# Expert layer of a two-layer vision tower: all experts for every token, or tokens sorted by expert into 73 blocks

## What is computed

```python
def _L1_ffn_ref(x, W_qkv, b_qkv, W_gate, b_gate, W_experts, b_experts):   # D = 256, E = 8, TOP_K = 2
    qkv = (x @ W_qkv + b_qkv).reshape(B, S, 3, H, hd)
    attn_out = softmax(q @ k / sqrt(hd)) @ v
    gate = jax.nn.softmax(x @ W_gate + b_gate, axis=-1)
    top_g, top_i = jax.lax.top_k(gate, TOP_K)
    combine = jnp.sum(jax.nn.one_hot(top_i, E) * top_g[..., None], axis=2)
    expert_out = jnp.einsum('bsd,edf->bsef', x, W_experts) + b_experts
    moe_out = jnp.einsum('bsef,bse->bsf', expert_out, combine)
    return attn_out + moe_out
h = h + _L1_ffn_ref(_layernorm(h), ...)
```

## Time and profile before

| what | value |
|---|---|
| median of 3 runs | 2212.42 us (2212.3 to 2214.53) |
| the profiled execution | 2215.91 us, its span 2214.1 us |
| mean granted PE clock | 0.957 |
| PE / DVE / ACT / POOL busy | 2060.5 / 1603.9 / 901.8 / 737.7 us |
| `pass_moe` | 1321 to 1736 us of the span |
| `pass_attend` | 1736 us to the end |

### The profile page before, as it was taken

The page is one execution under the profiler, slowest core; times in us unless marked ns, Lnnn a source line. Parts: engine busy times, 40 slices in busy tenths (PEclk is TensorE's granted clock), DMA queues, the critical chain, the costliest instruction groups (busy, mean ns, idle before and its releaser), DMA issues. The chain is left out here.

```text
span 2214.1 us, 36468 instructions
## 1 busy us (share of the span) xinstructions
PE 2060.5 (93%) x11553; PEld 1337.2 (60%) x11553; DVE 1603.9 (72%) x4388; ACT 901.8 (41%) x2108; POOL 737.7 (33%) x1355
## 2 busy tenths in 40 slices
PE   7997989998999998999979849999999999999997
PEld 5886753335888885777743227888888433333332
DVE  3335977774777767999948846767676888888881
ACT  1113655552112214444424411222222167777777
POOL 3553645553333332333311101111111523333332
PEclk9997989998999999999989969999999789999999
DMA  4332769872000000000010001121217213333310
GB/s 131 114 104 53 176 161 201 165 160 64 1 1 1 1 1 15 1 1 1 1 57 9 10 28 39 40 49 39 49 40 169 43 35 78 78 79 78 78 45 20
DMA packets 212523, 133.86 MB, mean 60 GB/s; under 512 B 113370, under 2 KB 201604, under 8 KB 212356
## 3 DMA queue, kind: packets, MB, share of 16 engines
q1 hardware_dynamic: 212356, 131.78, 25.4%
HBM read 89.96 MB, written 41.38 MB: 59 GB/s over the span
## 5 line engine op out<-in xcount | busy, mean ns | idle before, releaser
L2693 DVE TENSOR_REDUCE attend_mx<-ps 128x1 f32<-128x512 f32 x512 | 320.8, 681 | 40.3 <-PE ps L2387 39.2
L2530 ACT ACTIVATE attend_w<-ps 128x512 f32<-128x512 f32 x512 | 280.5, 596 | 92.6 <-PE ps L2401 91.1
L2003 PE MATMUL ps<-keep_early,moe_zT 128*128 128x256 f32 x1056 | 243.5, 384 | 4.4 <-DVE keep_h L2158 4.4
L2003 PEld LDWEIGHTS ps<-keep_early,moe_zT 128*128 128x128 f32 x1056 | 196.5, 191 | 40.0 <-DVE keep_h L2158 15.5
L2387 PE MATMUL ps<-keep_x,keep_o 96*128 96x512 bf16 x512 | 208.0, 411 | 7.2 <-DVE attend_mx L2693 5.3
L2401 PE MATMUL ps<-keep_o,keep_x 99*128 99x512 bf16 x512 | 191.6, 384 | 2.7 <-ACT attend_w L2530 2.7
L2158 DVE SCALAR_TENSOR_TENSOR keep_h<-ps,moe_g,keep_h 128x256 f32<-128x256 f32 x264 | 127.6, 483 | 61.6 <-PE ps L2003 53.7
L2387 PEld LDWEIGHTS ps<-keep_x,keep_o 96*128 96x128 bf16 x512 | 50.1, 98 | 183.3 <-DVE attend_mx L2693 136.1
L1003 DVE SCALAR_TENSOR_TENSOR keep_early<-ps,first_causal 128x512 f32<-128x512 f32 (+3 forms) x256 | 113.7, 484 | 48.0 <-PE ps L885 43.6
L981 POOL TENSOR_TENSOR keep_early<-keep_early,first_causal 128x128 f32<-128x128 f32 x256 | 113.2, 458 | 86.5 <-ACT keep_early L949 85.5
L1216 PE MATMUL ps<-mlp_zT,keep_early 128*128 128x128 f32 x1056 | 129.1, 281 | 8.0 <-ACT mlp_zT L1258 8.0
(11 more groups left out here) (341 smaller groups left out, 4110.0 us busy)
## 6 DMA issues: line engine op xcount, KB each, us to landing
tok_xin<-in_xk SPq DMA_DIRECT2D x64, 256.0 KB, 2.7
qk_parts<-qkv_parts SPq DMA_DIRECT2D x33, 384.0 KB, 3.2
qk_parts<-moe_parts SPq DMA_DIRECT2D x33, 384.0 KB, 3.2
keep_o<-qk_parts SPq DMA_DIRECT2D x16, 384.0 KB, 4.7
keep_x<-qk_parts SPq DMA_DIRECT2D x16, 384.0 KB, 5.8
v_all<-qkv_v SPq DMA_DIRECT2D x33, 136.0 KB, 3.3
v_all<-moe_v SPq DMA_DIRECT2D x33, 136.0 KB, 3.2
keep_early<-v_all SPq DMA_DIRECT2D x16, 272.0 KB, 6.8
```

The source lines that it names most:

```text
L2003: last = nc.tensor.matmul(ps[:, E0 + pair % 2, e % 2 * D:(e % 2 + 1) * D], zT[:, u, k * P:(k + 1) * P], we[e][:, k, :], start=(k == 0), st ...
L2530: nc.scalar.activation(w[:, j, kt % 2, :], ps[:, SC + (HG * k + j) % RING, :], ACT.Exp)\
L2693: nc.vector.tensor_reduce(mx[:, t, k:k + 1], ps[:, MX + (TB * k + t) % RING, :], AX, ALU.max)\
```

## The change

`pass_moe` no longer multiplies a tile with all experts. Per tile DVE finds the two largest logits and their experts (`rank`, `choose`), `weigh` keeps the two softmax weights in `env.gates`. PE counts, with triangular bf16 matrices, how many tokens before this one chose the same expert (`count`, `totals`), and DVE makes from it two row numbers in a table in DRAM, `sorted` (`places`). POOL issues two indirect transfers a tile that write the normalized rows there (`scatter`). The pipeline has four tiles in hand instead of two, and six buffers of normalized rows. After the last tile DVE works out, on one partition, for each of 73 slots its expert and its first row (`slots`). Then the 73 blocks of 128 rows are done in order: SP reads the row number into a register and loads the block, PE transposes it, DVE copies it to SBUF, ACT reads the expert's number and copies that expert's weights to a fixed place, PE multiplies, DVE reads the number too and adds the expert's bias, and SP stores the result over the block. In `pass_attend` POOL gathers each token's two result rows, weights them and adds them to `env.h`, two tiles a unit. In `pass_fp4` SP writes zeros over the whole table (44,160 rows of 1 KB) in three transfers. The loads of the attention stage are issued at tiles 13, 17, 21 and 25 (`LATE = 20`). The biases of the experts are loaded as one 1 MB transfer, replicated over the partitions, at the start of the stage.

```diff
@@ pass_fp4, SP
             env.ahead["scan"].start(sp)
+            sp.wait_ge(s_blank, 1)
+            runs = io["sorted"].rearrange("(p n c) d -> p n (c d)", p=P, c=BLANK)
+            n = runs.shape[1] // 3
+            zero = env.x[:, 0:BLANK, :].rearrange("p (a c) d -> p a (c d)", a=1)
+            for i in range(3):
+                sp.dma_start(runs[:, i * n:(i + 1) * n, :], zero.to_broadcast([P, n, BLANK * D])).then_inc(env.s_blank_z, 16)
@@ pass_moe
+CAP = (NT + 1) * P
+NSLOT = 2 * NT + E - 1
+ROWS = E * CAP + NSLOT * P
...
+    NZ, NW, NY = 6, 2, 3
...
@@ pass_moe, SP, after the loop over tiles
+            sp.wait_ge(s_slots, 1)
+            for i in range(NZ):
+                sp.wait_ge(s_scat[i], 32 * ((NT - i + NZ - 1) // NZ))
+            def fetch(j, row):
+                past(sp, s_dT, j - NY + 1)
+                sp.dma_start(zs[:, j % NY, :], io["sorted"][bass.ds(row, P), :]).then_inc(s_zs[j % NY], 16)
+            def put_back(j, row):
+                sp.wait_ge(s_y, j + 1)
+                sp.dma_start(io["sorted"][bass.ds(row, P), :], y[:, j % NY, :]).then_inc(s_yout[j % NY], 16)
+            rows = []
+            for j in range(NSLOT):
+                rows.append(sp.value_load(slot_row[0:1, j:j + 1], min_val=0, max_val=ROWS - P))
+                fetch(j, rows[j])
+                if j >= NY:
+                    put_back(j - NY, rows[j - NY])
...
@@ pass_moe, PE
-                for pair in range(3):
-                    experts(s, u, pair)
-                turn_gates(s, u)
-                experts(s, u, 3)
...
-                expert_bias(s)
+            for i in range(NT + 4):
+                if live(i):
+                    transposes(i)
+                if live(i - 1):
+                    gate(i - 1)
+                if live(i - 3):
+                    project(i - 3)
+                if live(i - 2):
+                    count(i - 2)
...
+                if i - 4 >= 1:
+                    class_scores(i - 4)
+            def turn(j):
+                pe.wait_ge(s_zs[j % NY], 16 * (j // NY + 1))
+                past(pe, s_dz, j - 1)
...
+            def expert(j):
+                pe.wait_ge(s_dz, j + 1)
+                pe.wait_ge(s_dW, j + 1)
+                past(pe, s_y, j - 1)
...
+            turn(0)
+            for j in range(NSLOT):
+                if j + 1 < NSLOT:
+                    turn(j + 1)
+                expert(j)
...
@@ pass_moe, ACT
+            for j in range(NSLOT):
+                e = act.value_load(slot_e[0:1, j:j + 1], min_val=0, max_val=E - 1)
+                past(act, s_dM, j - NW + 1)
+                nc.scalar.copy(w_now[:, j % NW, :, :].rearrange("p k d -> p (k d)"),
+                               we[:, bass.ds(e, 1), :].rearrange("p a f -> p (a f)")).then_inc(s_dW, 1)
...
@@ pass_moe, POOL
+            for i in range(NT + 3):
+                if live(i + 2):
+                    deviation(i + 2)
+                if live(i - 3):
+                    third(i - 3)
+                if live(i - 2):
+                    scatter(i - 2)
...
@@ pass_moe, DVE
+            for i in range(NT + 4):
+                if live(i - 1):
+                    rank(i - 1)
+                if live(i - 3):
+                    value(i - 3)
+                if live(i - 1):
+                    choose(i - 1)
+                if live(i + 2):
+                    stats(i + 2)
+                if live(i - 1):
+                    weigh(i - 1)
+                if live(i - 2):
+                    places(i - 2)
+                if live(i + 2):
+                    apply(i + 2)
+                if i - 2 == NT - 1:
+                    slots()
+                if live(i - 3):
+                    split(i - 3)
...
+            turned(0)
+            for j in range(NSLOT):
+                if j + 1 < NSLOT:
+                    turned(j + 1)
+                result(j)
...
@@ pass_attend, POOL, per unit
                 if x.has(1):
                     parts(x)
                     class_weights(x)
+                owed = [i for i in (2 * x.s, 2 * x.s + 1) if i < NT]
+                for i in owed:
+                    fetch(i)
                 if x.follows():
                     add(2 * x.n(2) - 1, 1, x.b(3), 2 * x.half(3) + 1)
                 if x.has(2):
                     add(2 * x.n(2), 0, x.b(2), 2 * x.half(2))
+                for i in owed:
+                    if x.has(2):
+                        pool.wait_ge(s_o, 2 * x.n(2) + 1)
...
+                    combine(i)
```

More of the change, by code:

```diff
@@ L1944, in pass_moe @@
-        s_E, s_acc, s_TC, s_cT, s_be, s_beh, c_g = (a.sem(n) for n in ("E", "acc", "TC", "cTs", "be", "beh", "c_g"))
-        s_out, s_vout = a.sems("out", 2), a.sems("vout", 2)
-        block = a.block()
-        GL, LATE = 9, 6
+        lg = a.sb("lg", [P, E])
+        top = a.sb("top", [P, E])
+        below = a.sb("below", [P, 2, E])
+        ex = a.sb("ex", [P, 2, E])
+        total = a.sb("total", [P, 2])
+        which = a.sb("which", [P, E], U32)
+        which_f = a.sb("which_f", [P, 2])
@@ new lines, in pass_moe @@
+        chosen = a.sb("chosen", [P, 3, 2, E], BF16)
+        place = a.sb("place", [P, 2, E])
+        place_f = a.sb("place_f", [P, 2])
+        tri = a.sb("tri", [P, 2, P], BF16)
+        start = a.sb("start", [1, 1, E], BF16)
+        one = a.sb("one", [1, P], BF16)
+        full = a.sb("full", [1, E, NT])
+        blocks = a.sb("blocks", [1, 3, E])
+        order = a.sb("order", [1, E, E])
+        room = env.heads.room
+        after = room.rearrange("p a t -> p (a t)")[0:1, 0:2 * NSLOT * E].rearrange("p (n j e) -> p n j e", n=2, e=E)
@@ new lines, in pass_moe @@
+        rs = a.sb("rs", [P, 2])
+        ve = a.sb("ve", [P, 2])
+        s_fold, s_kq, s_kq0, s_in = (a.sem(n) for n in ("fold", "kqs", "kq0", "in"))
+        s_stat, s_rs, s_z, c_ln, c_rs = (a.sem(n) for n in ("stat", "rss", "zs_", "c_ln", "c_rs"))
+        s_T, s_zT, s_g, s_mx, s_ex, s_qk, s_v, s_qkf, s_p0, s_rest, s_p1, s_p2, s_va, s_c, s_cs = (
+            a.sem(n) for n in ("T", "zTs", "gs", "mx", "exs", "qk", "vs", "qkfs", "p0", "rests", "p1", "p2", "va", "c", "cs"))
+        s_lg, s_chosen, s_count, s_place, s_all, s_n, c_g, c_w, c_p, c_n = (
+            a.sem(n) for n in ("lgs", "chosens", "count", "places", "all", "n", "c_g", "c_w", "c_p", "c_n"))
@@ L1963, in _ @@
                     env.heads.load_class(sp, io)
-                if 0 <= unit < 4:
-                    env.heads.load(sp, io, unit // 2, unit % 2, unit)
+                if unit >= 0 and unit % 4 == 0 and unit < 16:
+                    env.heads.load(sp, io, unit // 8, unit // 4 % 2, unit // 4)
+            sp.wait_ge(s_slots, 1)
[13 more added lines that the diff above has]
+                    put_back(j - NY, rows[j - NY])
+            for j in range(NSLOT - NY, NSLOT):
+                put_back(j, rows[j])
+            for i in range(NY):
+                sp.wait_ge(s_yout[i], 16 * ((NSLOT - i + NY - 1) // NY))
             for u in range(2):
@@ L2087, in third, with scatter @@
                     .then_inc(s_p2, 1)
[L2089 to L2094, removed]
+            def scatter(s):
+                pool.wait_ge(s_place, s + 1)
+                for j in range(2):
+                    nc.gpsimd.indirect_dma_start(io["sorted"], bass.IndirectOffsetOnAxis(ap=pos[:, s, j:j + 1], axis=0),
+                                                 z[:, s % NZ, :], None).then_inc(s_scat[s % NZ], 16)
+            pool.wait_ge(env.s_blank_z, 48)
+            for s in range(2):
+                deviation(s)
+            for i in range(NT + 3):
+                if live(i + 2):
[4 more added lines that the diff above has]
+                    scatter(i - 2)
         @block.vector
@@ L2132, in gate, with split @@
-                dve.sem_inc(s_comb, 1)
-            def split(s, u):
+            def split(s):
+                u = s % 2
                 dve.wait_ge(s_p0, s + 1)
```

382 lines of the change are left out of this document (253 added, 129 removed).

## The result

| | before | after |
|---|---|---|
| median, 4 runs each | 2213.3 us | 2299.1 us (2298.3 to 2300.2) |
| ratio, 95% interval | 1 | 1.0388 [1.0370, 1.0406] |
| span, mean granted clock | 2214.1 us, 0.957 | 2296.5 us, 0.914 |
| PE / DVE / ACT / POOL busy | 2060.5 / 1603.9 / 901.8 / 737.7 us | 1987.3 / 1541.6 / 934.9 / 949.0 us |

What follows compares the result with a forecast made beforehand. PE bound the 415 us expert stage, busy 403.7. New stage 233 + 5.3 + 5.3 + 157 + 3 = 403.5 us, 11.5 less; +4.7 elsewhere; net -7 from 2212.4 gives 2205 us, range 2140 to 2260.

Steps and rivals of the forecast that it cites:

- The beat of a tile: Expert stage, tile part: 6.2 us a tile, set by POOL's loop with DVE, 33 tiles making 205 us.
- a beat over 7.5: Sign set for a wrong prediction: a tile beat of under 5 or over 7.5 us.
- PE falls to its lower level there: Rival, block part: PE at its lower clock sets the beat at 2.7 us, total 2245 us; chance 0.18.
- 3.8 + 2T: Tile beat from POOL's loop with DVE: 3.8 us plus two scatters of T each, T taken as 1.2 us.
- The rival with scatters of 2.0 us: Slower rival, tile part: each scatter costs 2.0 us, 53 us more, total 2258 us; chance 0.13.
- that with 0.5: Faster rival: scatters of 0.5 us and row-number reads of 0.3 us, 61 us less, total 2144 us; chance 0.22.
- DVE's 4.9: Tile part: DVE's summed work a tile, 4.9 us, said not to set the beat.
- The table: Between tiles and blocks: 13 dependent DVE steps on one partition working out the blocks, 5.3 us.
- The block beat: Block part: three blocks share a round trip of 6.45 us, so 2.15 us a block, 73 blocks making 157 us.
- L = 1.0: Block part: SP's reading of a row number into a register takes 1.0 us.
- Attention: Attention stage: POOL's gathers and sums fit its idle gaps, costing 2 us in the first units; stage 434 +- 3 us.
- a unit over 27.2 us: Sign set for a wrong prediction: a longer attention unit would mean POOL's gaps don't hold the gathers.

Runs made afterwards that it cites:

- experiment 1: Changed kernel with VectorE's take_class(i-5) moved from the end to the start of its iteration: 2185.4 us, 0.9868 of the kernel before.
- experiment 2: Changed kernel with the class scores in two PSUM banks in turn, the copy staying last on VectorE: 2184.6 us, 0.9873 of the kernel before.
- experiment 5: Changed kernel with six more unread 128x256 products a tile on TensorE ahead of the class scores: 2227.2 us.
- experiment 3: Changed kernel without the two scatters of each tile, take_class left last: 2309.3 us.
- experiment 4: Changed kernel with take_class(i-5) first on VectorE and without the two scatters of each tile: 2164.0 us.
- experiment 7: Changed kernel with POOL's first combine of an attention slot put ahead of its second addition: 2290.2 us, 1.0339 of the kernel before.
- experiment 6: Changed kernel with four block buffers instead of three: 2288.5 us, 1.0331 of the kernel before.
- experiment 10: Changed kernel with take_class first, four block buffers, first combine between the additions, and block stores issued by GpSimd: 2148.2 us, 0.9706 of the kernel before.

## Why the prediction was wrong, step by step

- **The beat of a tile: failed, and it decides.** The step is "Neither sets the beat, because POOL now also issues two scatters a tile and its order ties it into a loop with DVE." I had added up PE's 4.3 to 4.7 us and DVE's 4.9 us as if they ran side by side, and had looked for a loop only where the change put a new operation. The loop between PE and DVE goes over the one bank of the class scores, an operation that the change did not touch, only moved: on PE to `i - 4`, on DVE to the end. I had asked of the scatters who waits behind them and had not asked it of the copy. What the runs showed in its place is a beat of 10.24 us, set by PE and DVE in turn; of the signs that I had set, a beat over 7.5 came true. The loop cost 4.16 us a beat: 114.7 us by the two tile parts (349.4 and 234.7), 114 and 115 by the medians of experiments 1 and 2. No rival of mine had it.
- **Its clock.** Of that, experiment 5, a single run, puts some 72 us to the lower level. My rival "PE falls to its lower level there" had the mechanism and the wrong place: in the blocks, where I had been afraid of it, the clock was 0.97.
- **3.8 + 2T and T: right.** The two scatters took 2.5 us with their gaps, a T of 1.25 for my 1.2, and the rest of the loop 3.6 for my 3.8: a beat of 6.08 for 6.2, once the other loop was out; experiments 3 and 4 show that POOL's loop binds only then. The rival with scatters of 2.0 us is out, and so is that with 0.5.
- **DVE's 4.9: near, in part by luck.** The beat of experiment 4 was 5.14 us with DVE busy for 4.9 of it, but 0.6 of that is one small step that POOL's third part holds up (below). Without it my sum was 0.6 too high.
- **The table: right**, 1647.7 to 1653.1, 5.4 us for 5.3.
- **The block beat: right in kind, mis-sized in two terms.** Three blocks do share a round trip, but it took 5.3 us (three beats of 1.77) and not 6.45: the landing 2.1 for my 3.0, and the row read with its address 0.77 for my L = 1.0. The 0.5 that I had taken off for what DVE's read hides stands on no row, and no run shows it. The Trainium skill (DMA: Bandwidth & Descriptors, Latency and other measured facts) gives a `tensor_load`, which is what the read is in the trace, a floor of about 0.6 us. The trace does not bear that out: 72 of SP's 73 reads took 0.27 to 0.29 us, the first 1.07, and the steps on registers behind a read 0.48. The part came 26 us shorter than forecast, 137.2 for 163. The loads behind the stores in SP's queue were no slower: both landed in about 2 us.
- **Attention: mis-sized, and from other causes.** The 434 us that I gave for the stage are the length of the window of the earlier trace rows; the stage lasts 477.6. I had forecast +2 at its start and there were +13.4. The start cost 0.6: the first split comes at 1836.85, 31.4 us into the stage against 25.5 before, but the second follows after 21.1 us instead of 26.3. The 14 units behind it cost 10.6, and that is DVE's small subtractions held up by POOL's multiply: experiment 7 took 9.7 us off the stage. The sign that I had set, a unit over 27.2 us, came true (27.76) and did not mean what I had said. The last 2.2 us come behind the last split, 48.4 us for 46.3, where the end of the kernel waits for a DRAIN instruction of POOL (last section). All this is one profile each; the same code took 489.5 to 496.4 us in the profiles of experiments 1 to 6.
- **The zeros: right.** Issued from 833.4 us on, the last landed by some 946 (issued at 856.7, at most 89.4 to land), where I had reckoned with 209 us, and DVE was busy for 258.3 us of the window 834 to 1131, for 258.2 before.
- **The late loads: 2 us forecast.** In the changed kernel nothing shows, since a beat of 10 us covers them. In experiment 1 the four beats with a load took 9.40, 9.17, 8.59 and 8.75 us instead of 6.08: 11.6 us, of which the next beats made up 1.5. A cover that a slow loop gives goes with the loop.

Net: +109 for the tile part, -26 for the blocks, +11 for the attention stage: 94 us, the distance from 2205 to 2299. The blocks hid part of the miss.

The design is worth what the likeliest case said, and more: with the loop open it gains 1.3%, some 29 us, where I had said 7, and with the edits of experiment 10 it gains 2.9%. But that is another kernel than the one that I forecast, and that it gains 22 us more than I had said is for the most part the work of the blocks, 26 us shorter than my sum.

## What to carry to other kernels

When each engine's order is written by hand, list for every bank or buffer with one copy who fills it and who empties it, and at which place in each engine's iteration: if the emptier stands behind work that needs the filler's same iteration, the two take turns and their times add. Do this for the operations that a change merely moves too. Here the pair also lost TensorE's upper clock (0.71 granted), so the price was more than the sum. The first sign in this profile was a stretch in which the busiest engine, PE, was busy for 68% and the granted clock was below 1.

## What was not expected of the hardware

- More work made the kernel faster: six useless products a tile, 72 us less, clock 0.71 to 1.00 (experiment 5).
- A step of 128x8 on DVE (L2271, one input) took 0.84 us in experiment 1, against 0.23 in the changed kernel, when it began beside POOL's third part, and it ended with it. The groups of the two kernels from 1400 to 1550 us, changed kernel first:

```profile
L2271 DVE TENSOR_SCALAR moe_below<-moe_top 128x8 f32<-128x8 f32 x14 | 3.2, 231 | 0.5
```

```profile
L2271 DVE TENSOR_SCALAR moe_below<-moe_top 128x8 f32<-128x8 f32 x21 | 17.6, 839 | 0.7
```

- A direct store on POOL's queue took 0.54 us to issue and 0.7 to the next; on SP's it was 0.36. Behind the last block DVE then stood idle for 9.6 us (experiment 10) instead of 3.1, though the last store landed within 2.0 us of its issue. What the engines waited for is in the trace: each stage ends with a DRAIN instruction on every engine, ahead of the barrier, and POOL's took 7.4 us. It took 0.7 to 1.5 us in every stage in which POOL had issued no transfer, the expert stage without scatters included (1.25, experiment 4), and 6.2 to 8.3 us in every stage in which it had. In the changed kernel the one of the expert stage is covered by the blocks, and the one at the end of the kernel is not. The rows of the end of the kernel before and after, and of the end of the expert stage in experiment 10 (ns, start in us):

```profile
L2271 POOLq DRAIN  x1: 821/821/821, 2208.6 to 2208.6; - x1
```

```profile
L2486 POOLq DRAIN  x1: 6223/6223/6223, 2288.8 to 2288.8; - x1
```

```profile
L1942 POOLq DRAIN  x1: 7423/7423/7423, 1651.9 to 1651.9; - x1
```

The last gather of the changed kernel was issued at 2258.3 us, 30 us before its last DRAIN, and POOL had added its rows, so this is no wait for a transfer to land; what the time goes to is left open.
